# Criss-cross attention on x itself, its weighted sum projected afterwards

## The reference

```
q = Wq x + bq          # 64 channels
k = Wk x + bk          # 64 channels
v = Wv x + bv          # 512 channels
energy_H[h,w,g] = q[:,h,w] . k[:,g,w]     (minus 1e30 where g == h)
energy_W[h,w,u] = q[:,h,w] . k[:,h,u]
att = softmax over the 192 energies of a position
out = gamma * (sum_g v[:,g,w] att_H[h,w,g] + sum_u v[:,h,u] att_W[h,w,u]) + x
```

## Time and profile before

| What | Value |
|---|---|
| Median of 3 timed runs | 4361.13 us (4360.35 to 4363.99) |
| Profiled execution, span from first to last instruction | 4357.4 us, 92393 instructions |
| Its time outside the span | not listed apart; the median of the runs is 3.7 us above the span |
| DMA | 947.78 MB, mean 218 GB/s |
| Store of a chunk of x, issue to landing | 6.3 us (median) |

### The profile page before, as it was taken

How to read it: one execution, slowest core, us unless ns; L and a number is a source line. 1 busy time by engine, 2 the same in 40 slices (tenths; PEclk the granted TensorE clock), 3 DMA queues, 4 the chain that set the end, 5 groups by cost and what they waited for, 6 DMA issues and landing times.

```text
span 4357.4 us, 92393 instructions
## 1 busy us (share of the span) xinstructions
PE 4063.6 (93%) x26136; PEld 3654.3 (84%) x26136; DVE 2184.9 (50%) x3932; ACT 1288.8 (30%) x2522; POOL 1148.6 (26%) x1006
## 2 busy tenths in 40 slices
PE   8989999898998999989999899997999979999897
PEld 7878988788887998879988699886988869988697
DVE  3348533485334853348433484335843358433584
ACT  3342133421334213341133411335113351133510
POOL 3322133221332213322233222332223322233211
PEclk9988999889998999979999799997999979999799
DMA  5548977489774897749977499774997749977499
GB/s 177 172 150 213 247 231 244 153 219 253 232 238 146 222 256 229 247 136 229 249 236 239 136 232 245 246 238 134 234 239 243 240 137 232 252 237 232 148 243 315
DMA packets 555124, 947.78 MB, mean 218 GB/s; under 512 B 45120, under 2 KB 383552, under 8 KB 533568
## 3 DMA queue, kind: packets, MB, share of 16 engines
q1 hardware_dynamic: 555072, 947.30, 75.2%
HBM read 550.77 MB, written 396.36 MB: 217 GB/s over the span
## 4 chain that ended last, share of the span: by engine, by line
PE 82%; DMA 9%; issue 3%; ACT 2%; SPq 1%; POOL 1%; DVE 0%; ACTq 0%; POOLq 0%; DVEq 0%
PE bank L708 36%; PE bank L766 26%; PE bank L724 9%; DMA Pe<-e_scratch 7%; PE bank L745 5%; PE bank L734 3%; PE bank L755 3%; ACT kq L461 1%; DMA KQ<-kq_scratch 1%; POOL Pe L388 1%; ACT E L466 1%; DMA kq_scratch<-kq 1%; POOL x_split L372 0%; SPq L224 0%; DVE X L608 0%
## 5 line engine op out<-in xcount | busy, mean ns | idle before, releaser
L708 PE MATMUL bank<-Wv_hi,x_split 128*128 128x512 f32 x4608 | 1525.6, 399 | 0.0
L766 PE MATMUL bank<-Pt,V 128*128 128x128 f32 x12288 | 1478.4, 280 | 0.0
L766 PEld LDWEIGHTS bank<-Pt,V 128*128 128x128 f32 x12288 | 1436.7, 196 | 0.0
L608 DVE TENSOR_TENSOR X<-bank,X 128x384 f32 (+1 forms) x1536 | 1115.4, 734 | 559.1 <-PE bank L766 559.0
L372 POOL TENSOR_TENSOR x_split<-X,x_split 128x768 fp32r<-128x768 f32 x384 | 702.3, 1854 | 1411.1 <-ACT x_split L435 1411.0
L555 DVE TENSOR_TENSOR v_out<-bank,bv_row 128x512 f32<-128x512 f32 x576 | 398.3, 691 | 1287.3 <-PE bank L708 1281.2
L708 PEld LDWEIGHTS bank<-Wv_hi,x_split 128*128 128x128 f32 x4608 | 867.9, 188 | 189.0 <-issue 0.5
L708 PE MATMUL bank<-Wv_lo,x_split 128*128 128x512 f32 x2304 | 912.5, 396 | 0.0
L388 POOL TENSOR_TENSOR Pe<-Pe,mx 96x384 f32<-96x384 f32 x384 | 316.6, 824 | 1288.6 <-DMA Pe<-e_scratch 1287.8
L474 ACT ACTIVATE Pt<-bank 96x384 f32<-96x384 f32 x384 | 187.3, 488 | 1424.9 <-PE bank L755 1424.9
L446 ACT ACTIVATE kq<-bank,bqk_sb 64x192 f32<-64x192 f32 x768 | 320.6, 417 | 812.1 <-PE bank L734 645.8
(11 more groups left out here) (45 smaller groups left out, 1551.9 us busy)
## 6 DMA issues: line engine op xcount, KB each, us to landing
V<-v_scratch SPq DMA_DIRECT2D x384, 768.0 KB, 5.7
X<-in_x SPq DMA_DIRECT2D x192, 768.0 KB, 5.1
v_scratch<-v_out SPq DMA_DIRECT2D x576, 256.0 KB, 3.8
out<-X SPq DMA_DIRECT2D x192, 768.0 KB, 6.3
Pe<-e_scratch SPq DMA_DIRECT2D x384, 144.0 KB, 5.3
kq_scratch<-kq SPq DMA_DIRECT2D x384, 96.0 KB, 2.3
e_scratch<-E SPq DMA_DIRECT2D x384, 72.0 KB, 1.7
e_scratch<-E SPq DMA_DIRECT2D x192, 144.0 KB, 1.9
```

Of the source, the lines that this page charges most:

```text
L608: nc.vector.tensor_tensor(xs, o_ps[r][:, :].rearrange("p (t n) -> p t n", t=CT)[:, :, 0:N], xs, ALU.add).then_inc(o_added, 1)
L708: last = nc.tensor.matmul(v_ps[t % 2][:, :], x_split[:, j, lo, ct, at], w[:, ct, :], start=(ct == 0 and n == 0), stop=(ct == CT - 1 and n ...
L766: last = nc.tensor.matmul(o_ps[r][:, ct * WIDE:(ct + 1) * WIDE], V[:, c, r, ct * P:(ct + 1) * P], Pt[:, c, r * N:r * N + WIDE], start=True ...
```

## The change

V isn't computed any more. The attention is a weighted sum of x itself, and Wv is applied to that sum: `Wv (sum of x att) + bv * gamma + x`. The gamma and the sum of exponentials are in the factors, as before, and both directions' weights of a position add up to gamma, which is why bv is multiplied by gamma once. So:

- x is given three times, in an order of its own each: by chunk (`x`), by position with the column first (`x_col`) and with the row first (`x_row`). The attention's operands XT are pieces of two columns or rows (384 KB) of these, in rings of six and three. The scratch of V and that of K and Q are gone. K and Q of a whole batch stay in SBUF (KQ).
- Y takes X's place. The column attention is moved from PSUM into Y, even columns by DVE, odd ones by ACT, in four instructions each; the row attention is added by DVE in rows. Y's chunk n+1 is then split into high and low parts (Sy, one buffer), projected in four groups of 12 matmuls with 384 columns, and written with x and the bias to chunk n, which is stored.
- Between the projections of chunks 7 to 18 lie K, Q and row energies of the next batch, two chunks each. Those of batch 0 are a stage ahead of all. The column energies are a stage behind each batch's rows, with K gathered by POOL.
- Pt isn't padded; the attention matmuls have 96 moving columns. Pt has two buffers and one PSUM bank for transposes. The low halves are made by POOL (first two channel tiles) and DVE (the other two).
- There are no hardware loops; the program is written out for all batches.

The core of the diff, removed lines:

```diff
-            def load_attention(b, along, p, c, free=False):
-                    sp.wait_ge(p_turned, past(p_turned, g - 2))
-                sp.dma_start(Pe[:, c, :, :], e_dram[along, b, :, at, :]).then_inc(p_in[c], 16)
-                    sp.wait_ge(o_summed, past(o_summed, (g - 2) * ROWS))
-                sp.dma_start(V[0:N, c, :, :], (v_by_row if along else v_by_column)[b, :, at, :])\
-                    .then_inc(v_in[c], 16)
-                        last = nc.tensor.matmul(o_ps[r][:, ct * WIDE:(ct + 1) * WIDE],
-                                                V[:, c, r, ct * P:(ct + 1) * P], Pt[:, c, r * N:r * N + WIDE],
-                                                start=True, stop=True)
```

SyncE, added:

```diff
+            def load_p(b, i):
+                along, n = i // CHUNKS, i % CHUNKS
+                sp.wait_ge(p_turned, past(p_turned, p_no(b, i - PRING)))
+                e_landed(sp, b, n if along else CHUNKS + n)
+                sp.dma_start(Pe[:, i % PRING, :, :], e_dram[along, b, :, n * ROWS:(n + 1) * ROWS, :])\
+                    .then_inc(p_in[i % PRING], 16)
+            def load_xtc(b, i):
...
+                    sp.wait_ge(o_summed, past(o_summed, o_no(b, (i - CRING) * PIECE + PIECE - 1)))
+                sp.dma_start(column_piece(i)[0:N, :, :], x_col[b, :, i * PIECE:(i + 1) * PIECE, :])\
+                    .then_inc(xtc_in[i % CRING], 16)
+            def column_stage(b):
+                load_xres(b, 0)
+                for i in range(RRING):
+                    load_xtc(b, i)
+                for i in range(PRING):
+                    load_p(b, i)
+                for i in range(RRING, CRING):
+                    load_xtc(b, i)
+                for g in range(CHUNKS):
+                    for i in (2 * g + CRING, 2 * g + CRING + 1):
+                        if i < PIECES:
+                            load_xtc(b, i)
+                        elif i < PIECES + RRING:
+                            load_xtr(b, i - PIECES)
+                    load_p(b, g + PRING)
```

ACT, DVE and POOL, the parts that the prediction speaks of:

```diff
+            def round_x(a, m, before=True):
+                act.wait_ge(xa_in[j], past(xa_in[j], 16 * (a * (CHUNKS // 2) + m // 2 + 1)))
+                act.wait_ge(qk_summed, past(qk_summed, a * CHUNKS + m))
+                for cts in halves:
+                    nc.scalar.activation(Sx[:, 0, cts, :], XA[:, j, cts, :], ACT.Copy).then_inc(x_hi_made, 1)
+            def round_y(b, n):
+                act.wait_ge(r_added, past(r_added, b * N + (n + 1) * ROWS))
+                act.wait_ge(proj_summed, past(proj_summed, (b * CHUNKS + n) * CT))
+                for cts in halves:
+                    nc.scalar.activation(Sy[:, 0, cts, :], Y[:, n + 1, cts, :], ACT.Copy).then_inc(y_hi_made, 1)
+            def move_column(b, i):        # ACT; DVE's has nc.vector.tensor_copy
+                act.wait_ge(o_summed, past(o_summed, o_no(b, i)))
+                to = Y[:, 1:, :, :].rearrange("p n t (r w) -> p t n r w", w=N)[:, :, :, :, i]
+                for t in range(CT):
+                    last = nc.scalar.activation(
+                        to[:, t, :, :], oc_ps[i % CBANKS][:, t * N:(t + 1) * N].rearrange("p (n r) -> p n r", r=ROWS),
+                        ACT.Copy)
+            def low_x(a, m):              # DVE, channel tiles 2 and 3; POOL has 0 and 1
+                nc.vector.tensor_tensor(Sx[:, 1, halves[1], :], XA[:, m % 2, halves[1], :],
+                                        Sx[:, 0, halves[1], :].bitcast(F32), ALU.subtract).then_inc(x_lo_b_made, 1)
+            def gather_k(a, g):           # POOL
+                src = KQ[0:CQ, :].rearrange("p (h w) -> p w h", w=N)[:, g * ROWS:(g + 1) * ROWS, :]
+                nc.gpsimd.tensor_copy(Kg[0:CQ, g % 2, :].rearrange("p (w h) -> p w h", w=ROWS), src)\
+                    .then_inc(k_gathered, 1)
```

DVE's order in the row stage (`a_now` holds the two chunks of the next batch, if any):

```diff
+                for n in range(CHUNKS):
+                    a_now = a_chunks(n) if more else []
+                    if more and n + 1 == A_FIRST:
+                        low_x(b + 1, 0)
+                    finish(b, n, 0)
+                    if a_now:
+                        shift(b + 1, a_now[0])
+                        low_x(b + 1, a_now[1])
+                    finish(b, n, 1)
+                    finish(b, n, 2)
+                    if a_now:
+                        sum_z(b + 1, a_now[0])
+                    finish(b, n, 3)
+                    if n + 1 < CHUNKS:
+                        low_y(b, n + 1)
+                    if n + 2 < CHUNKS:
+                        add_row(b, n + 2, 0)
+                        add_row(b, n + 2, 1)
+                    if a_now:
+                        shift(b + 1, a_now[1])
+                    if n + 2 < CHUNKS:
+                        add_row(b, n + 2, 2)
+                        add_row(b, n + 2, 3)
+                    if a_now:
+                        if a_now[1] + 1 < CHUNKS:
+                            low_x(b + 1, a_now[1] + 1)
+                        sum_z(b + 1, a_now[1])
```

TensorE's order in the row stage:

```diff
+                for n in range(CHUNKS):
+                    a_now = a_chunks(n) if more else []
+                    if a_now:
+                        project_kq(b + 1, a_now[0])
+                    project(b, n, 0)
+                    if a_now:
+                        row_energies(b + 1, a_now[0])
+                    project(b, n, 1)
+                    project(b, n, 2)
+                    if a_now:
+                        project_kq(b + 1, a_now[1])
+                    project(b, n, 3)
+                    if n + 3 < CHUNKS:
+                        turn(b, CHUNKS + n + 3)
+                    if n + 2 < CHUNKS:
+                        attend_row(b, n + 2, 0)
+                        attend_row(b, n + 2, 1)
+                    if a_now:
+                        row_energies(b + 1, a_now[1])
+                    if n + 2 < CHUNKS:
+                        attend_row(b, n + 2, 2)
+                        attend_row(b, n + 2, 3)
+                if more:
+                    for g in range(CHUNKS):
+                        column_energies(b + 1, g)
+                    turn_stats(b + 1)
+                    turn_factors(b + 1)
```

More of the change, by code:

```diff
@@ L96, in criss_cross_attention @@
[L96 to L109, removed]
@@ new lines, in p_no, with o_no, out_landed, e_landed @@
+        def p_no(b, i):
+            return b * (2 * CHUNKS) + i + 1
+        def o_no(b, i):
+            return b * (2 * N) + i + 1
+        def out_landed(eng, b, n):
+            eng.wait_ge(out_stored[n % 2], past(out_stored[n % 2], 16 * (b * (CHUNKS // 2) + n // 2 + 1)))
+        def e_landed(eng, a, i):
+            eng.wait_ge(e_stored[i % ERING], past(e_stored[i % ERING], 16 * (a * (2 * CHUNKS // ERING) + i // ERING + 1)))
+        def batches(eng, prologue, whole, last):
+            prologue()
+            for b in range(B - 1):
+                whole(b)
+            last(B - 1)
@@ new lines, in column_energies, with prologue @@
+            def column_energies(a):
+                gather_q(a, 0)
+                gather_q(a, 1)
+                for g in range(CHUNKS):
+                    if g + 2 < CHUNKS:
+                        gather_q(a, g + 2)
+                    exponentials(a, CHUNKS + g)
+            def prologue():
+                act.wait_ge(wqk_in, 16)
+                nc.scalar.activation(Wqk_hi[:, :, :], raw_qk[:, :, :], ACT.Copy).then_inc(w_hi_made, 1)
+                act.wait_ge(small_in, 48)
+                round_x(0, 0, before=False)
+                for m in range(CHUNKS):
+                    evict_kq(0, m, before=False)
+                    if m + 1 < CHUNKS:
+                        round_x(0, m + 1)
+                    if m:
+                        exponentials(0, m - 1)
+                exponentials(0, CHUNKS - 1)
+                column_energies(0)
+                factors(0)
@@ L692, in _, with whole, last @@
+            def whole(b):
+                column_stage(b)
+                row_stage(b, True)
+            def last(b):
+                column_stage(b)
+                row_stage(b, False)
+            batches(dve, prologue, whole, last)
         @block.tensor
         def _(pe):
[L694 removed]
+            for s in by_pe:
                 pe.sem_inc(s, START[s])
[L696 to L698 removed]
@@ new lines, in project @@
+            def project(b, n, c):
+                if c == 0:
+                    pe.wait_ge(y_lo_a_made, past(y_lo_a_made, b * CHUNKS + n + 1))
+                    pe.wait_ge(y_lo_b_made, past(y_lo_b_made, b * CHUNKS + n + 1))
+                pe.wait_ge(out_made, past(out_made, (b * CHUNKS + n) * CT + c - 1))
+                at = slice(c * P, (c + 1) * P)
+                for ct in range(CT):
+                    for k, (w, lo) in enumerate(((Wv_hi, 0), (Wv_hi, 1), (Wv_lo, 0))):
+                        last = nc.tensor.matmul(proj_ps[c % 2][:, 0:CP], w[:, ct, at], Sy[:, lo, ct, :],
+                                                start=(ct == 0 and k == 0), stop=(ct == CT - 1 and k == 2))
+                last.then_inc(proj_summed, 1)
```

(7 more changed lines are left out.)

1136 lines of the change are left out of this document (559 added, 577 removed).

## The result

The changed kernel takes 4854.15 us (median of 4 runs, 4833.12 to 4865.43), the kernel before 4361.82: ratio 1.112 [1.110, 1.115]. It is 11% slower; I had forecast 4700 us, 7.8% slower. The profiled execution took 4865.43 us for a span of 4863.6, so my 4696 us of span came out 168 us too small; by the medians it is 154.

A forecast was written before the change was run, and what follows sets the result against it. TensorE, busy for 93% of the span, bounds the kernel. Start 238, seven middle batches 4004 and last batch 454 make 4696 us of span, so 4700 us, 7.8% slower; own range 4560 to 4840, widened to 4300 to 4900.

The forecast's parts named there:

- Column attention: Column stage: the new queue order makes chunks wait for Pe; 4.72 us a chunk, 113 us for 24, bounds 94 to 132.
- Pe's path as written: Column stage: Pe's issue waits behind an x piece; then landing 3.75 us, scaling 0.82; 5.5 us from chunk end to turn.
- Attention matmuls: Both attention stages: 96 moving columns instead of 128 gain nothing; 0.1125 us a record, bounds 0.085 to 0.1125.
- Column energies and the way to the attention: Energies at DVE's pace, 1.85 us a group, 45 us; then 13 us from last shift to first attention matmul.
- Row stage: Row attention with projections and next K/Q: TensorE 365 us a batch plus 36 of waits and bank change, bounds 0 to 60.
- DVE has low Y until 3.1: Row-stage iteration: DVE finishes its low half of Y 3.1 us after the projection ends, ahead of adds and low x.
- The start: Batch 0's K/Q stage alone, in series through one Sx: 7.0 us a chunk, 168 us; 238 with loads and column energies.
- A: Rival, whole kernel: everything new is covered, Pe landing within some 2.3 us; 4267 us, 2% faster; chance 0.20.
- B: Rival, attention matmuls: moving columns set the price, 0.085 us a record; 4450 us, still slower; chance 0.13.
- C: Rival, instruction fetch: straight code for eight batches stops TensorE 0.5 us per 8 KB more; 4900 us; chance 0.07.
- D: Rival, column stage: moves out of PSUM bind at 0.6 us an instruction, 5.3 us a chunk; 4810 us; chance 0.08.

The follow-up runs named there:

- y_low_dve: Changed kernel with DVE making both low halves of y and POOL none; 4698.84 us, ratio 1.078 to the kernel before.
- y_serial: Changed kernel with one more wait: DVE starts its low half of y only when POOL's has been made; 4985.50 us, ratio 1.143.
- xa_early: Changed kernel with the first two x chunks of the next batch issued one row-stage iteration earlier; 4798.19 us, ratio 1.102.
- warm: Changed kernel with ten unused matmuls behind each K/Q chunk of batch 0's stage, for the clock only; 4870.56 us, ratio 1.117.
- best: Changed kernel with Pe issued earlier, low y on DVE alone, low x ahead of the shift, next x loaded earlier, two split buffers in the first stage; 4245.17 us.
- before_96: Kernel before with one edit: attention matmuls move 96 columns instead of 128; 4363.09 us, ratio 1.0008.
- p_early: Changed kernel with Pe's load issued ahead of the two x pieces in SyncE's column stage; 4700.21 us, ratio 1.079.

## Why the prediction was right, and where its sizes were off

- **Sign and range.** Slower, as the forecast said, and within 4300 to 4900, though 14 us above the forecast's own range of 4560 to 4840. The mechanisms are in the main the ones named; the sum was 168 us of span short: 20 in the start, 19 in each of seven middle batches (591.2 measured, 572 forecast), 13 in the last (512 against 499, its column energies included).
- **Column attention: right.** Forecast 4.72 us a chunk and 113 + 4 a stage; measured 4.9 and 112 to 122, 117.6 in the mean, by Pe's path as written, and its removal gave 154 us. In each stage one to three chunks also took over 5 us for their 32 records instead of 3.6, like the one shown above at a granted clock of 0.51; the sum didn't have them. Pe landed in 4.4 us by the median where I took 3.75.
- **Attention matmuls: right.** No gain from 96 moving columns; shown in the kernel before, and 3.57 to 3.59 us for 32 records in the changed one.
- **Column energies and the way to the attention: right as a sum, off in both parts.** DVE's three instructions follow one another without the gaps that I had added, so a group takes 1.58 us instead of 1.85, and POOL's gather (0.830) keeps up. From the first energy matmul to the last shift it is 39.6 us instead of 45, and from there to the first attention 16.1 instead of 13; 55 to 57 together against 58. That the sum is right is luck.
- **Row stage: the step that failed.** I gave it 32 us of waits beside TensorE's 365; it took 416 to 420, so 51 to 55. The K/Q iteration came out at its number (19.98 us against 12.41 + 5.6 + 1.9 = 19.9), in part by luck: TensorE waits 0.8 us for DVE's low x and not 1.9, and I had left out 0.5 for the add that row 3 of the attention needs, and 0.2 for POOL's low x. The term "DVE has low Y until 3.1" was too short: 1.94 us instead of about 1.3 beside POOL's half, which makes 13.66 instead of some 13.1 us of an iteration without K/Q, 7 a batch. y_low_dve and y_serial show that the cause is the two engines at once. I had seen the contention at the kernel's start and put 0.6 us in for it where a whole second instruction was due. Then x's load for the next batch, which I had left out: 8 a batch, shown by xa_early. Of the 6 a batch that are left, some 2 are the last chunk's projection: in the second batch its 48 records take 10.13 us instead of 8.37, behind 3.7 us without a matmul and at a granted clock of 0.82. The rest stays open.
- **The start: near its upper bound.** 213 us to the first column energies against 193; 8.0 us a chunk against 7.0, bounds 6.0 to 8.4. TensorE's clock was at 0.72 there; at 0.90, in warm, a chunk still takes 7.5. The mechanism, one split buffer and everything in series, holds: with two buffers and the right order in best, 4.7 us.
- **Rivals.** A, all covered, fell for this kernel, but what it described can be reached: with the waits mended it is 4245 us, and I had worked out 4267. B fell by before_96. C: instruction packets went from some 50 to 340, 4.67 MB in all, and the pieces of the chain that name no releaser ("issue") hold TensorE idle for 59 us in all, against 70 in the kernel before; the code cost nothing that can be seen. D fell: a record of a move out of PSUM lasts 0.321 us on DVE and 0.356 on ACT, four overlapping ones 0.83, below its 0.6 for each, and p_early's chunks of 3.90 us show them covered.

## What to carry to other kernels

An issue put behind a wait in a shared queue costs the wait, whatever the transfer takes; ask of each DMA what stands ahead of it and who still needs it. VectorE and GpSimd, sharing a subtraction of two SBUF operands in halves, took as long as VectorE alone for both, so a split between these two has to be measured before it is believed. Edits that relieve the second-latest thing show nothing alone: before discarding one, try it with the first mended.

## What the runs showed of the hardware

- A 128x768 two-input subtraction on DVE takes 0.96 to 0.97 us alone and 1.94 when it begins beside POOL's of the same size, which keeps its 1.81; POOL's 96x384 multiply goes from 0.83 to 1.54 behind a DVE one. In every pair looked at here the cost fell on the one that began later.
- Pe, 144 KB, landed in 2.2 us at least and in 4.4 and 5.0 by the median in two orders of the same loads; the order with the longer landing was 154 us faster.
- A 128x96 copy from PSUM with strided output shows 0.32 us on DVE and 0.36 on ACT; the records overlap, and four in a row take 0.83 on either.
- Behind 1.60 us without a matmul the granted clock was 0.51 for the next 6.5 us, and 32 attention records took 6.60 us instead of 3.59; behind 0.36 and 0.46 us without one it had stayed at 1.00.
